# Distances for the sort's permutation matrices: from six biased squares on ScalarE to a TensorE difference and one square

## The reference

```
edge_index = stack([src, dst])
x = _layernorm(x + _L0_gnn_ref(x, edge_index, edge_type_64, ...))
x = _layernorm(x + _L1_gnn_ref(x, src, dst, edge_weight, ...))
x = _layernorm(x + _L2_gnn_ref(x, edge_index, edge_type_2, ...))
x = _layernorm(x + _L3_gnn_ref(x, edge_index, ...))
```

## Time and profile before

| | before |
|---|---|
| median of 3 runs | 4126.3 us (4124.19 to 4128.95) |
| the profiled execution | 4132.2 us, span 4130.5 us |
| PE busy | 3511.6 us, 85% |
| DVE busy | 3204.4 us, 78% |
| ACT busy | 2337.2 us, 57% |
| POOL busy | 391.8 us, 9% |

### The profile page before, as it was taken

How to read it: one execution, slowest core, us unless ns; L and a number is a source line. 1 busy time by engine, 2 the same in 40 slices (tenths; PEclk the granted TensorE clock), 3 DMA queues, 4 the chain that set the end, 5 groups by cost and what they waited for, 6 DMA issues and landing times. The chain is left out here.

```text
span 4130.5 us, 90438 instructions
## 1 busy us (share of the span) xinstructions
PE 3511.6 (85%) x36615; PEld 2901.3 (70%) x36740; DVE 3204.4 (78%) x3960; ACT 2337.2 (57%) x5142; POOL 391.8 (9%) x336
## 2 busy tenths in 40 slices
PE   2666777776999999869999999996999999967776
PEld 1555666664666666569999999995888888845554
DVE  7999999998777777589999999996666666723233
ACT  4998999996555555423333333334666666634343
POOL 3003211122111111100000000001000000000000
PEclk9999999997999999879999999998999999989999
DMA  3000000001322222200000000002333333268988
GB/s 107 2 2 2 2 2 2 2 2 37 114 110 110 111 111 110 77 2 2 2 2 2 2 2 2 2 2 85 99 101 101 99 101 103 86 116 170 168 170 172
DMA packets 423099, 257.10 MB, mean 62 GB/s; under 512 B 329994, under 2 KB 419863, under 8 KB 422548
## 3 DMA queue, kind: packets, MB, share of 16 engines
q1 hardware_dynamic: 422196, 248.79, 22.7%
q10 hardware_dynamic: 480, 2.40, 0.2%
HBM read 86.93 MB, written 85.49 MB: 42 GB/s over the span
## 5 line engine op out<-in xcount | busy, mean ns | idle before, releaser
L97 DVE TENSOR_TENSOR both_hot<-iota_own,recs 128x1792 bf16<-128x1792 bf16 (+1 forms) x686 | 754.4, 1107 | 231.5 <-PE rR L1466 121.9
L1830 ACT ACTIVATE gC<-qC 128x896 f32<-128x896 f32 x343 | 314.7, 918 | 647.6 <-PE qC L1850 647.6
L1862 PE MATMUL qO<-A,gC 128*128 128x132 f32 x4802 | 615.3, 280 | 0.0
L1862 PEld LDWEIGHTS qO<-A,gC 128*128 128x128 f32 x4802 | 566.6, 190 | 0.0
L1474 PE MATMUL rO<-sl_f,terms 128*128 128x384 bf16 (+1 forms) x1934 | 476.4, 355 | 3.7 <-DVE A L1242 2.2
L2174 ACT ACTIVATE some_r<-rC 128x512 fp32r<-128x512 f32 (+1 forms) x686 | 336.4, 543 | 252.6 <-PE rC L2204 252.1
L628 PE MATMUL pV<-VO,PM 128*128 128x70 bf16 (+4 forms) x6524 | 259.8, 199 | 236.2 <-ACT PM L484 159.7
L1432 ACT ACTIVATE sl_f<-rC 128x896 bf16<-128x896 f32 x343 | 313.8, 915 | 255.2 <-PE rC L1454 254.4
L2454 PE MATMUL tO<-tables_r,Xr 128*128 128x448 f32 x1372 | 357.6, 392 | 116.5 <-ACT tables_r L2322 80.1
L91 DVE TENSOR_TENSOR PM<-iota_b,place 128x2944 bf16<-128x2944 bf16 (+2 forms) x226 | 410.4, 1816 | 30.8 <-ACT place L464 30.4
L1466 PE MATMUL rR<-rel_hot,both_hot 128*128 128x65 bf16 x2450 | 410.9, 194 | 25.5 <-DVE A L1242 12.2
(11 more groups left out here) (298 smaller groups left out, 6225.4 us busy)
## 6 DMA issues: line engine op xcount, KB each, us to landing
tables<-sl_f SPq DMA_DIRECT2D x343, 224.0 KB, 1.9
sl_f<-tables SPq DMA_DIRECT2D x343, 224.0 KB, 2.5
sl_f<-tables SPq DMA_TRANSPOSE x343, 3.7
edges<-terms SPq DMA_DIRECT2D x1, 3528.0 KB, 11.2
B<-in_x SPq DMA_DIRECT2D x1, 2744.0 KB
out<-B SPq DMA_DIRECT2D x7, 392.0 KB
terms<-in_edge_type ACTq DMA_DIRECT2D x2, 686.0 KB
terms<-in_edge_weight ACTq DMA_DIRECT2D x1, 686.0 KB
```

The source lines that it names most:

```text
L97: return v.tensor_tensor(o.rearrange("p n k (a b) -> p (n k) a b", b=2), iota_own[:, 0:w].rearrange("p (a b) -> p a b", b=2).unsqueeze(1). ...
L1862: mm = pe.matmul(pO[i % SUMS][:, 0:XW], Cs[:, U % 2, j, :], A[:, a, :], start=a == 0, stop=a == NT - 1)
```

## The change

What `distances` squares is now made by TensorE. A new step `apart_from(n)` writes to a new PSUM tile `pZ` (two banks) the difference place - iota of ACT's columns: a unit matrix times `place`, broadcast over 128 numbers, plus a negative unit matrix times `iota_b`, in groups of up to four columns. `distances(n)` is one activation that squares all of them out of PSUM. The share of level 3 goes from 4 to 5 columns. GpSimd makes the two matrices. And ACT's order in the loop is another: paired(n), looked(n+1), evict(n-1), distances(n), then as before. `pD`, used once at the end, shares the bank of `pW`.

```
-            SHARE = (6, 5, 4)
+            SHARE = (6, 5, 5)
+            whole_b = sb("whole_b", [P, P], BF16, c1)
+            minus_b = sb("minus_b", [P, P], BF16, c1)
-            pD = ps("pD", [P, 512], c1)
+            pZ = ps("pZ", [P, 8, P], c1)
+            pD = pW
...
+                    gp.tensor_scalar(whole_b[:, :], ident_f[:, :], 1.0, None, ALU.mult).then_inc(consts, 1)
+                    gp.tensor_scalar(minus_b[:, :], ident_f[:, :], -1.0, None, ALU.mult).then_inc(consts, 1)
...
                     def distances(n):
+                        act.wait_ge(s_far, n + 1)
                         if n >= 1:
                             act.wait_ge(s_rest_perm, n)
-                        for j in range(share):
-                            col = cols - share + j
-                            ins = act.activation(apart_b[:, j, :], iota_b[:, 0:P], ACT.Square, scale=-1.0, bias=rank[:, n % 2, col:col + 1])
-                        ins.then_inc(s_pair, 1)
+                        act.activation(apart_b[:, 0:share, :], pZ[:, 0:share, :], ACT.Square).then_inc(s_pair, 1)
...
                             paired(n)
-                            distances(n)
+                            if n > a and n + 1 < b:
+                                looked(n + 1)
                             if n > a:
                                 evict(n - 1)
+                            distances(n)
...
                             near(n)
-                            if n + 2 < b:
-                                looked(n + 2)
...
+                    def apart_from(n):
+                        u = units[n]
+                        cols, share = u.npos * u.ngrp, SHARE[u.level - 1]
+                        pe.wait_ge(s_pair, 2 * n + 1)
+                        for a in range(0, share, 4):
+                            w = min(4, share - a)
+                            held = place[:, n % 2, cols - share + a:cols - share + a + w, 0:1].broadcast_to([P, w, P])
+                            pe.matmul(pZ[:, a:a + w, :], whole_b[:, :], held, start=True, stop=False, skip_group_check=True)
+                            mm = pe.matmul(pZ[:, a:a + w, :], minus_b[:, :], iota_b[:, 0:P].unsqueeze(1).broadcast_to([P, w, P]), start=False, stop=True, skip_group_check=True)
+                        mm.then_inc(s_far, 1)
...
                         for n in range(a, b):
+                            apart_from(n)
                             if n + 2 < b:
                                 count(n + 2)
```

More of the change, by code:

```diff
@@ L198, in gnn_four_layers_kernel @@
             pV = [ps(f"pV{i}", [P, 512], c1) for i in range(2)]
-            pD = ps("pD", [P, 512], c1)
+            pZ = ps("pZ", [P, 8, P], c1)
             pL = ps("pL", [P, 2, P], c1)
             pW = ps("pW", [P, 512], c1)
+            pD = pW
             names = ("loads", "pads", "consts", "tri_made", "prep", "fields", "blanks", "packed", "s_pad0", "s_load0", "s_xin0", "s_stored", "turned", "wt_made",
-                     "s_dup", "s_hot", "s_cnt", "s_look", "s_taken0", "s_more", "s_pair", "s_val", "s_perm", "s_rest_perm", "s_out", "s_ev",
+                     "s_dup", "s_hot", "s_cnt", "s_look", "s_taken0", "s_more", "s_pair", "s_val", "s_perm", "s_rest_perm", "s_far", "s_out", "s_ev",
                      "s_tp0", "s_xt0", "s_y0", "s_own0", "s_high0", "s_rest0", "s_mid0", "s_low0", "s_wt0", "s_total", "s_words", "s_named", "s_kind", "s_left", "s_last")
             (loads, pads, consts, tri_made, prep, fields, blanks, packed, s_pad, s_load, s_xin, s_stored, turned, wt_made,
-             s_dup, s_hot, s_cnt, s_look, s_taken, s_more, s_pair, s_val, s_perm, s_rest_perm, s_out, s_ev,
+             s_dup, s_hot, s_cnt, s_look, s_taken, s_more, s_pair, s_val, s_perm, s_rest_perm, s_far, s_out, s_ev,
              s_tp, s_xt, s_y, s_own, s_high, s_rest, s_mid, s_low, s_wt, s_total, s_words, s_named, s_kind, s_left, s_last) = [sem(n, c1) for n in names]
@@ L373, in _ @@
                     gp.tensor_scalar(lift[:, :], ident_f[:, :], LIFT, None, ALU.mult).then_inc(consts, 1)
-                    gp.wait_ge(consts, 12)
+                    gp.tensor_scalar(whole_b[:, :], ident_f[:, :], 1.0, None, ALU.mult).then_inc(consts, 1)
+                    gp.tensor_scalar(minus_b[:, :], ident_f[:, :], -1.0, None, ALU.mult).then_inc(consts, 1)
+                    gp.wait_ge(consts, 14)
                     def low_parts(m):
@@ L630, in route @@
                         mm.then_inc(s_out, 1)
-                    pe.wait_ge(consts, 12)
+                    pe.wait_ge(consts, 14)
                     for a, b in phases:
@@ L702, in _ @@
                     v.wait_ge(prep, PREP)
-                    v.wait_ge(consts, 12)
+                    v.wait_ge(consts, 14)
                     def hot(n):
```

## The result

The changed kernel takes 4144.6 us (median of 6 runs, 4138.2 to 4150.6) against 4126.2 us (6 runs, 4124.2 to 4130.6): ratio 1.0042, 95% interval 1.0029 to 1.0055. The forecast was 4145 us. A second copy of the same kernel, run later, gave 4144.0 us and 1.0043 (1.0031 to 1.0055). The profiled execution has a span of 4140.0 us and a mean granted clock of 0.972; before it was 4130.5 us and 0.963.

A forecast was written before the change was run, and what follows sets the result against it. VectorE was taken to bound level 1 at 4.10 us a unit, until a new loop through TensorE takes over at 4.49. Terms 18.7 - 1 - 5 + 3 + 1 + 1.5 = +18.2 us put the median at 4145 us, range 4112 to 4168.

The forecast's parts named there:

- The chain's length: Level 1: the loop route, four matmuls, square, `double`, `near`, back to route sums to 4.49 us a unit.
- The square's price: ScalarE's square out of PSUM: about 0.81 us for 768 numbers, 0.70 for 640, holding ScalarE for 0.71 and 0.60.
- The rival with the slow read: TensorE reads the broadcast operand at twice the time a column: +125 us, 4270 us; chance 0.04.
- VectorE's wait: Level 1: VectorE idles 0.4 us a unit, put down to `place` or `VO`'s wait for a route.
- The boundary: Unit 48 to 49, between level 1 and level 2: no cost forecast, 0.
- Units 49 to 76: Stretch without side work, VectorE above the chain: -5 us of 6.6 us of waits.
- Units 77 to 209: Levels 2 and 3: waits for `place` go, waits for TensorE replace them; 54.7 us a round against 54.8, -1 us.
- a late `place`: Levels 2 and 3: record activations delay `place`, adding 0.6 and 0.4 us to a round's 53.7.
- TensorE's clock: Rival: once in 14 units the granted clock falls, costing some 1.4 us a time, 12 times: 4162 us; chance 0.13.
- The end of the sort: Units 210 to 216: VectorE's round already shorter than the chain, matmuls at half speed, 0.5 us a unit: +3 us.
- the start: Before unit 0: two new GpSimd constants +1 us, first route later at TensorE's lower clock +1.5 us.
- The level 1 term: Level 1: the chain replaces VectorE's 4.10 us round, 0.39 us a unit for 48 units: +18.7 us.

The follow-up runs named there:

- order_back: Changed kernel with ScalarE's order of before (evict between the square and `near`): 4197.4 us, ratio 1.0170.
- apart_ahead: Changed kernel with TensorE making the distances of unit n+1 before it routes n, and the evict behind the square: 4124.9 us, ratio 0.9993.
- matmuls_unread: Changed kernel with the squares, shares and ScalarE order of before; TensorE still makes `pZ`, which nobody reads or waits for: 4116.4 us, ratio 0.9977.
- double_ahead: Changed kernel with `double` ahead of the square on ScalarE: 4121.3 us, ratio 0.9985.
- after_share4: Changed kernel with the old shares (6, 5, 4) instead of (6, 5, 5): 4145.2 us, ratio 1.0037.
- order_alone: Kernel before with the changed kernel's ScalarE order alone, no matmuls, squares and shares as they were: 4246.2 us, ratio 1.0292.
- count_between: Changed kernel with `count(n + 2)` ahead of `apart_from(n)` on TensorE: 4576.0 us, ratio 1.1086.
- by_phase_8: Changed kernel; level 1: matmuls before route, evict behind square, eight ScalarE columns instead of six; levels 2 and 3: `double` before square. 4129.0 us, ratio 1.0000.

## Why the prediction was right, and where it was not

**What bounds level 1.** Right: ScalarE's relief is real (40 us of 140) and worth nothing, since VectorE set the pace and only the new chain could change it. `order_back` (+0.32 for 0.31 us put into the chain) and `apart_ahead` (back to 4.10 with the chain open) show both halves. `matmuls_unread` shows that the same matmuls cost level 1 nothing while the chain is open.

**The chain's length.** Right in the sum, 4.49 us forecast and measured, and in its terms to within 0.04 us: route 1.29, matmuls 0.65 and 0.20, square 0.71, `double` 0.46, `near` 0.92, to the route 0.29. The square's price was the one term without a row of its kind. From 68 us to the end of the sort, ScalarE's groups by line (busy us, mean ns, idle before):

```profile
L478 ACT ACTIVATE apart_b<-pZ 128x640 bf16<-128x640 f32 (+1 forms) x226 | 164.4, 727 | 45.7 <-PE pZ L627 42.3
```

It takes 811 ns for 768 and 704 ns for 640 numbers. The page of the Trainium skill that I had set beside it ("ScalarE: Activation LUTs", What ACT_TABLE_LOAD costs) gives 826 ns for the first without its 93 ns for an operand as bias, and 919 with it; the trace agrees with the first, less 15 ns. (Of the earlier trace rows I had written that they give 826 too; by their slope they give 809, and the sum went by that.)

**The broadcast operand.** A matmul whose moving operand repeats one number 128 times starts the next one 0.21 us on, for 512 columns (165.82 to 166.03), as the one beside it that reads `iota_b` does (0.22). The rival with the slow read falls.

**VectorE's wait.** The 0.4 us are there, but not where I had put them: neither `place` nor `VO` waits, `hot` does, for `double`'s copy (9.6 us in 32 waits from 100 to 240 us). It changes no number.

**The boundary.** Missed, 2.0 us, and 4.1 in the second copy. I had counted periods, and a phase's end isn't one: the last route waits for the chain's `near`, 4.18 us behind `equal` instead of 2.13, with no next unit to hide it.

**Units 49 to 76.** The gain was 2.2 and not 5 us. I took the waits for `place` as if nothing came in their stead. In the changed kernel from 297 to 421 us they are nearly gone, as forecast:

```profile
DVE PM L91 <- ACT place L469: 1.0, 3, 0.4
```

What came in their stead is on VectorE itself. In this stretch some of its instructions run beside GpSimd's (L381 and L383 before, L386 and L388 now) and take far longer than the 1.67 to 1.69 us that such an `equal` has alone. One before, and one now:

```profile
308.27 2.50 DVE L91 TENSOR_TENSOR PM<-iota_b,place 128x2944 bf16<-128x2944 bf16 x1 [0.96 <-ACT place L464]
```

```profile
338.39 3.29 DVE L91 TENSOR_TENSOR PM<-iota_b,place 128x2944 bf16<-128x2944 bf16 x1
```

Before, 17 instructions are lengthened by 18.0 us in all; in the changed kernel, where more of VectorE's work falls beside GpSimd's, 18 by 22.2 us (21.5 in the second copy). That takes back about 4 of the 5 us. It is a reading of the timelines; no run moved GpSimd's work.

**Units 77 to 209.** A gain of 7.6 us where I had 1: a term mis-sized. My chain gave 53.7 us a round, and on it I had put 1.0 us for a late `place`; the rounds take 53.9. The waits of the changed kernel from 422 to 929 us have

```profile
ACT apart_b L478 <- PE pZ L627: 20.0, 102, 0.3
DVE PM L91 <- ACT place L469: 8.9, 18, 0.8
```

VectorE still waits for `place`, 8.9 us between units 77 and 209 where it was 19.8, and 4.1 us for `double`'s copy have come in; but the rounds lie only 0.2 us above the chain's 53.7: what I had added to the chain for the late `place` was too much by 0.8 a round. And TensorE's clock no longer falls in them (1.00 from 422 to 929 us). `matmuls_unread` has that too, with the old squares and a gain of the same size. How the 7.6 us divide between the relief of ScalarE, the third share and the clock was not taken apart. That the chain and not VectorE sets these rounds, the step on which the sign rested, is shown by `double_ahead` (52.9) and `after_share4` (no loss with a longer `equal`).

**TensorE's clock.** The rival had the fall of the clock stay and cost 1.4 us each time. Instead it went away: 1.00 in the round shown, against 0.97 before. What the rival feared is real, though, where the chain is longer: `order_alone` and `count_between`.

**The end of the sort.** +4.4 against +3, and +3.2 in the second copy.

The total came out to within 1 us because errors of both signs met: 1.5 less at the start and 6.6 and 0.7 less in the rounds and level 1 against 2 more at the boundary, 2.8 less of a gain in units 49 to 76 and 1.4 more at the end. That makes 15.5 us, 16.3 to the start of the next block (14.3 in the second copy), where 18.2 were forecast; the median lies 18.4 above that of before, 17.3 by the ratio. The level 1 term carries the sign and was right by itself; the agreement of the total is partly luck.

## What to carry to other kernels

Before work moves from a busy engine to an idle one, write down the loop that it closes: every instruction of both queues from the producer round to itself, with the signals between them, and compare that sum, not the busy shares, with the period of the engine that sets the pace. Then break the loop by the order in each queue, phase by phase, and look for the next loop each time before filling the room that is won (`by_phase_8`). And time the small parts of a change alone: here one digit alone gave about 10 us, and the whole cost 18.

## What was not expected of the hardware

Matmuls that nobody reads shortened the kernel by 10 us (0.9977), with the granted clock at 0.99 instead of 0.96 between 400 and 920 us. In `order_alone` and `count_between`, with TensorE left waiting 1.7 and 2.4 us a unit, 0.75 and 0.78 were granted in level 1, and routes of 1.44 us took up to 2.40; but `order_back`, which waits up to 1.7 us too, was granted 1.00, so the wait by itself doesn't tell. An `equal` of 1.68 us took up to 3.41 beside GpSimd's instructions between units 49 and 77. And a stage that no edit touches took 706 us in one execution and 712 in another of the same kernel, at 1.00 and 0.98 granted; a comparison of the spans of two single profiles would have shown 9.5 us where the sort had lost 16.3.
